# Query stages of a two-layer transformer kernel: order and engine of the weight splits, and loading of the input

## Chip, cores, metric

The kernel runs on one core of one Trainium2 chip. The metric is the device time of one execution in microseconds, the median of several runs.

## The reference

x has 256 tokens (8 sequences of 32) of 512 values. Six blocks are added to it, each on the layer-normalised x. Two of them, the first and the fourth, are cross-attention to a context of 512 positions per sequence, with 32 query heads and 8 key/value heads of 128:

```python
q = (latents @ Wq).reshape(bsz, q_len, HEADS, HEAD_DIM).transpose(0, 2, 1, 3)
k = (kv @ Wk).reshape(bsz, kv_len, KV_HEADS, HEAD_DIM).transpose(0, 2, 1, 3)
v = (kv @ Wv).reshape(bsz, kv_len, KV_HEADS, HEAD_DIM).transpose(0, 2, 1, 3)
q = rms_norm(q, q_norm_w)
k = rms_norm(k, k_norm_w)
...
x = x + _L0_xattn_ref(_layernorm(x, axis=-1), ctx_4096, L0_xattn_Wq, ...)
...
x = x + _L1_xattn_ref(_layernorm(x, axis=-1), ctx_4096, mask_1x1xSxS2_ff0, L1_xattn_Wq, ...)
```

In the first block the latents themselves are keys and values too (`kv` is the context followed by them); the fourth has a mask instead. Everything is float32.

## The kernel before

Each block is a stage, and each stage closes before the next opens. A cross-attention has three: `queries` (tiles named c0q and c1q), `attend` (c0a, c1a) and `project_out`. A float32 product is made of three passes on TensorE (`mm3`, lines 53 to 55), with each operand split in a high part (a copy by ScalarE to fp32r) and a low part (raw minus high, a subtraction). So each weight has to be split before it is used.

`queries` first normalises and transposes x (`LayerNormT`) and splits it (xT). Then Wq goes by in NQ = 8 tiles of 128x2048 (512 output columns, 1 MB) through a two-slot stage (`WeightStream`). For each tile there are TT = 2 projections n (128 tokens each) of 12 matmuls into one of SLOTS = 4 PSUM banks. Each projection n is followed by a chain: ScalarE squares (L490), VectorE sums (L565), GpSimd makes rstd (L406, L409), VectorE normalises into xn (L573), TensorE transposes (L450), ScalarE places the result into qT (L503). LAG = 2 says how many projections later TensorE does the transposes. In c0q four more projections of the latents (keys) with the same chain follow, then four of the latents' values without it, which are stored to DRAM.

Every engine works through its own list in order. In one tile ScalarE's order is: high part of the next wq tile (L194), high part of one key/value weight half (L520), then for each projection square and placing. VectorE's: low part of the next wq tile (L200), then sums and normalise for each projection. GpSimd's: rstd for each projection, then the low part of a key/value half (L413). The key/value weights are four columns of 128x2048 (two for keys, two for values); each is loaded and split in two halves, one per wq tile, so that all four are ready when the stage ends. SyncE's queue: norm weights, then in each tile wq and a key/value half; the context tiles of the first sequence follow the first pair; in c1q the first two wq tiles are already there. The eight tiles are written as a first pair, a loop over two pairs and a last pair (`peeled`). In the last tile both engines split the four context tiles (L273, L278).

`attend` works in 16 units of four context tiles. In a unit without scores yet (the first one) TensorE projects keys (column hf), transposes the normalised keys of the tile before (L831) and projects values (column 2 + hf); the chain of the keys is that of the queries (ScalarE L935, VectorE L1022, GpSimd L753 and L756, VectorE L1038, TensorE L831, ScalarE L906, VectorE L963). With k = 3 its own transposes follow its value projection at once.

`build_program` loads x and the identity in a block of its own, which all engines leave together once both have landed (lines 2213 to 2218), and then opens c0q.

## Time and profile before

| | |
|---|---|
| Runs | 1652.61 us median of 3 (1651.95 to 1656.21) |
| Profiled execution | 1653.78 us, of which span 1651.1 us |
| PE busy | 1524.9 us (92%) |
| DVE busy | 909.1 us (55%) |
| ACT busy | 642.6 us (39%) |
| POOL busy | 374.0 us (23%) |
| Mean granted clock of PE | 0.972 |
| c0q | 5 to 104 us |
| c1q | 816 to 889 us |

PE is TensorE, PEld its weight loads, DVE VectorE, ACT ScalarE, POOL GpSimd, SP SyncE; a q behind the name (PEq, SPq) is the engine's sequencer. A line of a timeline gives the start in us, the length in us, engine, line of the code, operation, output and inputs with their shapes, how many were merged, and in brackets how long the engine was idle before it and what released it. In the busy time by stretch each engine has its busy us and (in brackets) its instructions, then come PE's granted clock (1.00 is 2.4 GHz, 0.50 is 1.2 GHz), the share of time in which the DMA engines were busy, and GB/s. At the very start of c0q the column of the clock reads 1.00 while matmuls take 0.63 us instead of 0.39.

### The profile page before, as it was taken

What the parts mean: (1) busy time and instruction counts of PE and PEld (TensorE: products, weight loads), DVE (VectorE), ACT (ScalarE), POOL (GpSimd) and SP (SyncE); (2) the same over time, 40 slices, a digit from 0 to 9 for tenths busy, and PEclk for the clock granted to TensorE, in tenths of its full rate; (3) what the DMA queues carried; (4) which work ended last, traced back from release to release, by engine and by line L of the source; (5) the groups of instructions that cost most, each with busy time, mean ns of one, the idle gap of its engine ahead of it and who ended that gap; (6) DMA issues with size and microseconds to landing.
All of it is one profiled execution on the core that took longest, in us unless ns stands there. A gap on an engine that the chain in (4) does not pass through costs nothing. (4 is left out here: it accounts for less than half of the span.)

```text
span 1651.1 us, 24177 instructions
## 1 busy us (share of the span) xinstructions
PE 1524.9 (92%) x8362; PEld 1292.3 (78%) x8362; DVE 909.1 (55%) x1707; ACT 642.6 (39%) x1168; POOL 374.0 (23%) x510
## 2 busy tenths in 40 slices
PE   6899999999999998978797999999999999875898
PEld 4678888888888886777576888888888888654787
DVE  5724555555555555575564455555555554547565
ACT  4623343433433434453363333333333333421343
POOL 2622222222122221052355221122222111101000
PEclk9999999999999999989899999999999999988899
DMA  7210000010000111264160000000000001220442
GB/s 251 94 61 20 17 31 17 17 32 14 24 24 11 36 57 52 102 230 154 57 238 7 20 8 25 19 6 25 13 13 25 10 16 74 106 96 1 154 152 90
DMA packets 27371, 99.05 MB, mean 60 GB/s; under 512 B 4977, under 2 KB 5105, under 8 KB 22609
## 3 DMA queue, kind: packets, MB, share of 16 engines
q1 hardware_dynamic: 27312, 98.29, 17.0%
q8 instruction: 34, 0.56, 0.1%
q14 instruction: 25, 0.20, 0.0%
HBM read 95.66 MB, written 2.62 MB: 60 GB/s over the span
## 5 line engine op out<-in xcount | busy, mean ns | idle before, releaser
L53 PE MATMUL c1a_kbanks<-c_wkv_lo_r,c_cT_hi 128*128 128x512 f32 x256 | 106.4, 416 | 3.5 <-PEq L371 3.5
L53 PE MATMUL c0a_kbanks<-c_wkv_lo_r,c_cT_hi 128*128 128x512 f32 x256 | 106.1, 414 | 2.8 <-PEq L371 2.8
L1022 DVE TENSOR_REDUCE c1a_ss<-c1a_sq 128x4 f32<-128x512 f32 x64 | 43.8, 685 | 111.5 <-ACT c1a_sq L935 111.5
L753 POOL TENSOR_TENSOR c1a_ms<-c1a_ss,c1a_const 128x4 f32<-128x4 f32 x64 | 12.7, 199 | 395.2 <-DVE c1a_ss L1022 395.2
L753 POOL TENSOR_TENSOR c0a_ms<-c0a_ss,c0a_const 128x4 f32<-128x4 f32 x64 | 12.7, 199 | 393.4 <-DVE c0a_ss L1022 393.4
L55 PE MATMUL c0a_kbanks<-c_wkv_hi,c_cT_lo_r 128*128 128x512 f32 x256 | 101.2, 395 | 0.0
L55 PE MATMUL c1a_kbanks<-c_wkv_hi,c_cT_lo_r 128*128 128x512 f32 x256 | 100.9, 394 | 0.0
L54 PE MATMUL c0a_kbanks<-c_wkv_hi,c_cT_hi 128*128 128x512 f32 x256 | 100.7, 394 | 0.0
L53 PE MATMUL c0a_vbank<-c_wkv_lo_r,c_cT_hi 128*128 128x512 f32 x256 | 100.6, 393 | 0.0
L54 PE MATMUL c1a_kbanks<-c_wkv_hi,c_cT_hi 128*128 128x512 f32 x256 | 100.5, 392 | 0.0
L54 PE MATMUL c0a_vbank<-c_wkv_hi,c_cT_hi 128*128 128x512 f32 x256 | 100.4, 392 | 0.0
L1022 DVE TENSOR_REDUCE c0a_ss<-c0a_sq 128x4 f32<-128x512 f32 x64 | 43.9, 685 | 102.0 <-ACT c0a_sq L935 93.5
L55 PE MATMUL c1a_vbank<-c_wkv_hi,c_cT_lo_r 128*128 128x512 f32 x256 | 100.0, 391 | 0.0
L53 PE MATMUL c1a_vbank<-c_wkv_lo_r,c_cT_hi 128*128 128x512 f32 x256 | 99.9, 390 | 0.0
L55 PE MATMUL c0a_vbank<-c_wkv_hi,c_cT_lo_r 128*128 128x512 f32 x256 | 99.8, 390 | 0.0
L54 PE MATMUL c1a_vbank<-c_wkv_hi,c_cT_hi 128*128 128x512 f32 x256 | 99.6, 389 | 0.0
L993 DVE COPY c0a_pT<-c0a_ptbank 128x512 f32<-128x512 f32 x62 | 42.9, 692 | 97.8 <-PE c0a_sbank L807 97.8
L917 ACT ACTIVATE c1a_p<-c1a_sm,c1a_nmax 128x512 f32<-128x512 f32 x64 | 46.4, 725 | 128.4 <-DVE c1a_nmax L980 128.4
L917 ACT ACTIVATE c0a_p<-c0a_sbank,c0a_nmax 128x544 f32<-128x544 f32 x62 | 44.4, 716 | 125.8 <-DVE c0a_nmax L973 125.8
L935 ACT ACTIVATE c1a_sq<-c1a_kbanks 128x512 f32<-128x512 f32 x64 | 38.3, 598 | 128.7 <-PE c1a_kbanks L55 128.7
L935 ACT ACTIVATE c0a_sq<-c0a_kbanks 128x512 f32<-128x512 f32 x64 | 38.3, 598 | 119.5 <-PE c0a_kbanks L55 119.5
L993 DVE COPY c1a_pT<-c1a_ptbank 128x512 f32<-128x512 f32 x62 | 42.9, 692 | 75.0 <-PE c1a_ptbank L804 74.8
(469 smaller groups left out, 4417.9 us busy)
## 6 DMA issues: line engine op xcount, KB each, us to landing
g_stage<-in_l_wq SPq DMA_DIRECT2D x16, 1024.0 KB, 4.9
c_cT_lo<-in_ctx SPq DMA_DIRECT2D x64, 256.0 KB, 2.5
c_wkv_lo<-in_l_wo SPq DMA_DIRECT2D x16, 1024.0 KB, 4.9
e_stage<-in_e_w SPq DMA_DIRECT2D x20, 768.0 KB, 4.2
c_wkv_lo<-in_l_wkv SPq DMA_DIRECT2D x16, 512.0 KB, 5.6
m_stage<-in_mix_ffn SPq DMA_DIRECT2D x10, 768.0 KB, 4.5
c_vlat<-vlat_dram SPq DMA_DIRECT2D x32, 64.0 KB, 1.9
m_traw<-in_mix_out SPq DMA_DIRECT2D x1, 1792.0 KB, 12.9
```

The lines of the kernel that those rows point to most:

```text
L53: nc.tensor.matmul(out, a[0], b[1], start=start, stop=False)
L54: nc.tensor.matmul(out, a[0], b[0], start=False, stop=False)
L55: return nc.tensor.matmul(out, a[1], b[0], start=False, stop=stop)
L753: nc.gpsimd.tensor_tensor(ms[:, k % 2, :], ss[:, k % 2, :], const[:, 1, :], ALU.add).then_inc(k_mean, 1)
L917: nc.scalar.activation(dst, src, ACT.Exp, bias=nmax[:, k:k + 1], accum_out=rsum[:, k:k + 1]).then_inc(p_ready, 1)
L935: nc.scalar.activation(sq[:], kbank[k % 2], ACT.Square, scale=HD ** -0.5).then_inc(k_squared, 1)
L993: last = nc.vector.tensor_copy(pT[:, k % 2, :, :], bank[:, :].rearrange("p (t n) -> p t n", t=CT))
L1022: nc.vector.tensor_reduce(ss[:, k % 2, :], sq[:, :].rearrange("p (h d) -> p h d", h=UNIT_H), AX.X, ALU.add).then_inc(k_summed, 1)
```

## The change

- `WeightStream`: each wq tile is split in two halves of 1024 columns, each with its own high part on ScalarE and low part on VectorE. The low part of the first half can start when its high part is done. Both halves still stand ahead of the tile's squares and sums.
- `KeyValueWeights`: the four columns are loaded whole (1 MB each, one semaphore each) beside wq tiles 1 to 4, in the order 0, 1, 2, 3 (c0q) or 0, 2, 1, 3 (c1q). Their halves are split after the second projection of the tiles 3 to 6 (columns one and two of that order). The other two columns follow in c0q beside the four latent projections, in c1a beside the four context tiles of the first unit (`LATE`). The low parts are made by VectorE, no longer by GpSimd; TensorE waits for each column where it first uses it.
- LAG is 3.
- The tiles are written out, without a loop.
- x and ident are loaded at the head of c0q's own queue, with a semaphore each; only VectorE waits for x and only TensorE for ident. The block of its own is gone. The norm weights come behind the first wq tile, the context tiles behind the sixth.
- TensorE's first projections wait for their own half of xT, not for both.
- The split of the context moves: in c0q beside the value projections, in c1q two tiles behind each projection of the last tile.

```diff
...
@@ -171,41 +171,81 @@
 class WeightStream:
...
+    def load(self, sp, src, n):
+
+        need(sp, self.lo_ready, 2 * (n - 1))
+        sp.dma_start(self.stage[:, n % 2, :], src).then_inc(self.loaded[n % 2], 16)
...
+    def make_hi(self, act, n, half, used, per_tile):
+
+        if half == 0:
+            need(act, self.loaded[n % 2], (n // 2 + 1 - self.early) * 16)
+            need(act, used, per_tile * (n - 1))
+        self.nc.scalar.activation(self.part(self.split[0], n, half), self.part(self.stage, n, half),
                                   ACT.Copy).then_inc(self.hi_ready, 1)
...
+    def make_lo(self, dve, n, half):
+        dve.wait_ge(self.hi_ready, 2 * n + half + 1)
+        self.nc.vector.tensor_tensor(self.part(self.split[1], n, half), self.part(self.stage, n, half),
+                                     as_f32(self.part(self.split[0], n, half)),
                                      ALU.subtract).then_inc(self.lo_ready, 1)
...
+    def wait_tile(self, pe, n):
+        pe.wait_ge(self.lo_ready, 2 * n + 2)
...
+    def part(self, ap, n):
...
+    def load(self, sp, i):
+        sp.dma_start(self.raw[:, self.order[i], :], self.src[self.order[i]]).then_inc(self.loaded[i], 16)
+
+    def make_hi(self, act, n):
+        act.wait_ge(self.loaded[n // self.HALVES], 16)
+        self.nc.scalar.activation(self.part(self.split[0], n), self.part(self.raw, n),
+                                  ACT.Copy).then_inc(self.hi_ready, 1)
+
+    def make_lo(self, dve, n):
+        dve.wait_ge(self.hi_ready, n + 1)
+        self.nc.vector.tensor_tensor(self.part(self.split[1], n), self.part(self.raw, n),
+                                     as_f32(self.part(self.split[0], n)), ALU.subtract).then_inc(self.lo_ready, 1)
+
+    def wait_column(self, pe, col):
+        pe.wait_ge(self.lo_ready, self.HALVES * (self.order.index(col) + 1))
+
+    def column(self, col):
+        return tuple(h[:, col, :] for h in self.split)
 
...
-    SLOTS, LAG = 4, 2
+    SLOTS, LAG = 4, 3
+    KV_AT = NQ - 1 - 2 * kvw.HALVES
...
+        def kv_half(n):
+
+            h = n // TT - KV_AT
+            return h if n % TT == 1 and 0 <= h < 2 * kvw.HALVES else None
...
-                sp.dma_start(nk[:, 0:2], w["norm"]).then_inc(small_loaded, 16)
-
-                def step(i):
-                    for slot in range(2):
-                        if not (w["preloaded"] and is_at(i, 0)):
-                            stream.load(sp, w["wq"][bass.ds(2 * i + slot, 1), :, :]
-                                        .rearrange("a p n -> p (a n)"), i, slot)
-
-                        need(sp, wkv_loaded, 16 * (2 * i + slot))
-                        sp.dma_start(wkv_half(2, i, slot).rearrange("p a n -> p (a n)"),
-                                     w["wkv"][bass.ds(i, 1), :, slot * WKH:(slot + 1) * WKH]
-                                     .rearrange("a p n -> p (a n)")).then_inc(wkv_loaded, 16)
-                    if is_at(i, 0):
+                if first:
+                    sp.dma_start(x[:], g["a"]["x"].rearrange("(t p) d -> p t d", p=P)).then_inc(g["x_loaded"], 16)
+                    sp.dma_start(ident[:], g["a"]["ident"]).then_inc(g["ident_loaded"], 16)
+                for n in range(NQ):
+                    if first or n >= 2:
+                        stream.load(sp, w["wq"][n], n)
+                    if n == 0:
+                        sp.dma_start(nk[:, 0:2], w["norm"]).then_inc(small_loaded, 16)
+                    if 1 <= n <= 4:
+                        kvw.load(sp, n - 1)
+                    if n == 5:
                         for k in range(CT):
                             context.load(sp, 0, k)
-                peeled(sp, NQ // 2, step)
...
-                def wkv_lo_of(i, slot):
-                    nc.gpsimd.tensor_tensor(wkv_half(1, i, slot), wkv_half(2, i, slot),
-                                            as_f32(wkv_half(0, i, slot)), ALU.subtract).then_inc(wkv_lo, 1)
...
-                peeled(pool, NQ // 2, step)
-                pool.wait_ge(wkv_hi, NQ)
-                wkv_lo_of(NQ // 2 - 1, 1)
...
             @block.tensor
             def _(pe):
+                if first:
+                    pe.wait_ge(g["ident_loaded"], 16)
                 ln.tensor(pe)
-                ln.wait_ready(pe)
 
...
-                peeled(pe, NQ // 2, step)
+                for n in range(N0):
+                    tile, t = divmod(n, TT)
+                    if tile == 0:
+                        pe.wait_ge(ln.lo_ready, t + 1)
+                    if t == 0:
+                        stream.wait_tile(pe, tile)
+                    need(pe, normed, n - SLOTS + 1)
+                    project(t, stream.tile(tile), pbank[n % SLOTS]).then_inc(projected, 1)
+                    transposes(n - LAG)
...
+                            transposes(NN - LAG + j)
...
-                    transposes(n, n % SLOTS)
+                    transposes(n)
...
-                stream.make_hi(act, 0, 0, projected, TT)
+                for half in range(2):
+                    stream.make_hi(act, 0, half, projected, TT)
                 ln.scalar(act)
...
                 act.wait_ge(norm_ready, 2)
...
+                for n in range(N0):
+                    tile, t = divmod(n, TT)
+                    if t == 0 and tile + 1 < NQ:
+                        for half in range(2):
+                            stream.make_hi(act, tile + 1, half, projected, TT)
+                    square(n)
+                    place(n - LAG)
+                    if kv_half(n) is not None:
+                        kvw.make_hi(act, kv_half(n))
+                    if tile == NQ - 1 and not NL:
+                        for k in (2 * t, 2 * t + 1):
+                            context.make_hi(act, 0, k)
+                for j in range(NL):
+                    square(N0 + j)
+                    place(N0 + j - LAG)
+                    kvw.make_hi(act, 2 * kvw.HALVES + j)
...
+                        context.make_hi(act, 0, j)
                         act.wait_ge(vl_proj, j + 1)
                         if j == 0:
-                            act.wait_ge(stream.lo_ready, NQ)
+                            act.wait_ge(stream.lo_ready, 2 * NQ)
...
-                    stream.make_lo(dve, 0, 0)
+                    for half in range(2):
+                        stream.make_lo(dve, 0, half)
+                if first:
+                    dve.wait_ge(g["x_loaded"], 16)
                 ln.vector(dve, between)
...
+
+                for n in range(N0):
+                    tile, t = divmod(n, TT)
+                    if t == 0 and tile + 1 < NQ:
+                        for half in range(2):
+                            stream.make_lo(dve, tile + 1, half)
+                    sums(n)
+                    normalise(n - 1)
+                    if kv_half(n) is not None:
+                        kvw.make_lo(dve, kv_half(n))
+                    if tile == NQ - 1 and not NL:
+                        for k in (2 * t, 2 * t + 1):
+                            context.make_lo(dve, 0, k)
+                for j in range(NL):
+                    sums(N0 + j)
+                    normalise(N0 + j - 1)
+                    kvw.make_lo(dve, 2 * kvw.HALVES + j)
+                normalise(NN - 1)
+                if NL:
...
+                        context.make_lo(dve, 0, j)
...
+    EARLY = kvw.HALVES * (4 if tail else 2)
+    LATE = kvw.HALVES * 4 - EARLY
...
+                            kvw.wait_column(pe, hf)
                         project(k, hf, kbank[k % 2]).then_inc(k_proj, 1)
                         if lag:
...
+                            kvw.make_hi(act, EARLY + k)
 
                         if hf == 1 and k > 0 and not is_at(b, B - 1):
...
+                            kvw.make_lo(dve, EARLY + k)
                         if lag:
                             ot_place(a - 1, lb, lhf, lk, obank)
...
         stored = s.sem("stored")
         SEMAPHORES.clear()
-        with nc.Block() as block:
-            @block.sync
-            def _(sp):
-                sp.dma_start(x[:], a["x"].rearrange("(t p) d -> p t d", p=P)).then_inc(loaded, 16)
-                sp.dma_start(ident[:], a["ident"]).then_inc(loaded, 16)
-                sp.wait_ge(loaded, 32)
         L0 = {"wkv": a["l0_wkv"], "wq": a["l0_wq"], "wo": a["l0_wo"], "norm": a["l0_norm"], "ctx": a["ctx"], "mask": None,
```

## Rows read from the trace of the kernel before

**Rows 1.** Busy time by stretch (start:end in us, length, engines, clock, DMA).
```profile
46.45:54.19 7.74, 6.95 (x32) 5.25 (x33) 5.60 (x6) 5.10 (x6) 4.76 (x6) 1.00 0.53 197
84.30:87.50 3.20, 3.20 (x18) 2.65 (x17) 1.38 (x2) 1.18 (x2) 2.51 (x5) 1.00 0.02 5
11.00:14.00 3.00, 0.00 (x0) 0.00 (x0) 1.80 (x1) 2.14 (x3) 0.00 (x0) 1.00 0.98 396
824.00:832.00 8.00, 8.00 (x30) 6.38 (x29) 3.20 (x3) 2.36 (x4) 1.21 (x2) 0.81 1.00 376
```

**Rows 2.** Timeline of PE (transposes in c0q) and of ACT (end of c0q).
```profile
46.45 0.66 PE L450 MATMUL c0q_tbank<-g_ident,c0q_xn 128*128 128x128 f32 x4 [1.06 <-DVE c0q_xn L573]
...
100.32 0.60 ACT L543 ACTIVATE g_stage_r<-c0q_pbank 128x512 fp32r<-128x512 f32 x1 [2.10 <-PE c0q_pbank L55]
...
103.04 0.60 ACT L543 ACTIVATE g_stage_r<-c0q_pbank 128x512 fp32r<-128x512 f32 x1 [2.12 <-PE c0q_pbank L55]
```

**Rows 3.** Timeline of DVE: splits of wq tiles in c0q.
```profile
26.64 2.29 DVE L200 TENSOR_TENSOR c0q_w_lo<-g_stage,c0q_w_hi 128x2048 fp32r<-128x2048 f32 x1 [0.52 <-ACT c0q_w_hi L194]
...
33.40 4.07 DVE L200 TENSOR_TENSOR c0q_w_lo<-g_stage,c0q_w_hi 128x2048 fp32r<-128x2048 f32 x1 [1.27 <-ACT c0q_w_hi L194]
...
42.04 3.17 DVE L200 TENSOR_TENSOR c0q_w_lo<-g_stage,c0q_w_hi 128x2048 fp32r<-128x2048 f32 x1 [1.89 <-ACT c0q_w_hi L194]
```

**Rows 4.** Timeline of POOL: one rstd and one key/value subtraction in c0q.
```profile
25.94 1.01 POOL L409 TENSOR_TENSOR c0q_rstd<-c0q_ms,c0q_const 128x4 f32<-128x4 f32 x1
...
32.92 2.40 POOL L413 TENSOR_TENSOR c_wkv_lo_r<-c_wkv_lo,c_wkv_hi 128x1024 fp32r<-128x1024 f32 x1
```

**Rows 5.** Timeline of ACT: high parts of a wq tile and a key/value half.
```profile
47.83 1.91 ACT L194 ACTIVATE c0q_w_hi<-g_stage 128x2048 fp32r<-128x2048 f32 x1
49.63 1.05 ACT L520 ACTIVATE c_wkv_hi<-c_wkv_lo  x1
```

**Rows 6.** Timeline of SPq, ACT, DVE and PE at the start of c0q.
```profile
5.32 0.42 SPq L187 DMA_DIRECT2D g_stage<-in_l_wq  x1
...
10.26 1.91 ACT L194 ACTIVATE c0q_w_hi<-g_stage 128x2048 fp32r<-128x2048 f32 x1 [4.04 <-DMA g_stage<-in_l_wq]
...
12.20 2.29 DVE L200 TENSOR_TENSOR c0q_w_lo<-g_stage,c0q_w_hi 128x2048 fp32r<-128x2048 f32 x1 [3.31 <-ACT c0q_w_hi L194]
...
15.74 0.79 PE L53 MATMUL c0q_pbank<-c0q_w_lo,c0q_xT_hi 128*128 128x512 f32 x1 [5.54 <-DVE c0q_xT_lo L137]
...
21.03 0.59 PE L53 MATMUL c0q_pbank<-c0q_w_lo,c0q_xT_hi 128*128 128x512 f32 x1
```

**Rows 7.** Timeline of PE, ACT and POOL: start and end of c1q.
```profile
823.49 0.80 PE L53 MATMUL c1q_pbank<-c1q_w_lo,c1q_xT_hi 128*128 128x512 f32 x1 [2.14 <-DVE c1q_xT_lo L137]
...
883.16 0.60 ACT L490 ACTIVATE c1q_sq<-c1q_pbank 128x512 f32<-128x512 f32 x1 [1.23 <-PE c1q_pbank L55]
...
887.88 0.69 ACT L503 ACTIVATE c_qT<-c1q_tbank,c1q_norm 128x512 f32<-128x512 f32 x1 [0.57 <-PE c1q_tbank L450]
...
886.38 4.64 POOL L413 TENSOR_TENSOR c_wkv_lo_r<-c_wkv_lo,c_wkv_hi 128x1024 fp32r<-128x1024 f32 x2
...
891.37 0.76 PE L53 MATMUL c1a_kbanks<-c_wkv_lo_r,c_cT_hi 128*128 128x512 f32 x1 [3.52 <-PEq L371]
```

**Rows 8.** DMA issues of 0 to 30 us (KB each, median us to landing).
```profile
g_x<-in_x SPq DMA_DIRECT2D x1, 512.0 KB, 3.6
```

**Rows 9.** Busy time in one microsecond at the start of c1a.
```profile
893.00:894.00 1.00, 1.00 (x3) 0.78 (x3) 0.00 (x0) 0.00 (x0) 0.00 (x0) 0.50 0.43 117
```

**Rows 10.** Timeline of ACT, DVE and PE in the first unit of c1a.
```profile
902.60 0.60 ACT L935 ACTIVATE c1a_sq<-c1a_kbanks 128x512 f32<-128x512 f32 x1
...
905.50 0.69 DVE L1038 TENSOR_TENSOR c1a_kn<-c1a_kbanks,c1a_rstd 128x512 f32<-128x512 f32 x1 [1.47 <-POOL c1a_rstd L756]
...
907.40 0.60 PE L831 MATMUL c1a_ktbank<-g_ident,c1a_kn 128*128 128x128 f32 x4
...
918.08 0.66 PE L831 MATMUL c1a_ktbank<-g_ident,c1a_kn 128*128 128x128 f32 x4 [1.39 <-DVE c1a_kn L1038]
```

More of the change, by code:

```diff
@@ L171, with __init__ @@
 class WeightStream:
-    def __init__(self, nc, s, name, width, stage=None, split=None, preloaded=False):
-        self.nc, self.width, self.ahead = nc, width, int(preloaded)
-        self.stage = stage if stage is not None else s.sb(name + "_stage", [P, 2, width])
-        self.split = split if split is not None else s.pair(name, [P, 2, width])
+    def __init__(self, nc, s, name, width, stage, early):
+        self.nc, self.early, self.half = nc, early, width // 2
+        self.stage = stage
+        self.split = s.pair(name, [P, 2, width])
         self.loaded = [s.sem(f"{name}_loaded{i}") for i in range(2)]
```

203 lines of the change are left out of this document (71 added, 132 removed).

## Prediction

> **What bounds the kernel now.** I read the page first: TensorE is busy 92% of the span and its chain holds the end, so only TensorE's idle time, or its time at the low clock, can be won. The diff touches the two query stages (c0q, 5 to 104 us; c1q, 816 to 889 us), what lies before the first, and the first unit of the attention after each. The busy time by stretches comes next [rows 1]: one weight tile (two projections, two groups of transposes) takes 7.74 us, while the latent part of the same stage does one projection with its transposes in 3.20 us with TensorE busy throughout, so 6.40 us for the same work. The timeline of TensorE says who holds it [rows 2]: once per tile it waits 1.06 us for xn, the normalised queries that VectorE writes. What makes VectorE late stands in its own timeline [rows 3]: the split of the next weight tile takes 2.29 us undisturbed, but 3.17 and 4.07 us where GpSimd subtracts for the key/value weights (2.40 us each [rows 4]). It can start only when ScalarE has written the high part, 1.91 us, behind which ScalarE writes a key/value half for another 1.05 us before it squares [rows 5]. With LAG 2 the transposes come one projection too early for this chain.
>
> **The edits, costed.**
>
> *Tiles of c0q and c1q.* The key/value subtraction leaves GpSimd for VectorE. VectorE's tile was 5.60 us of work; now it is 5.60 - 3.17 + 2.29, and in the tiles 3 to 6 one key/value half more. That half on VectorE is not in the trace; it lies between half of 2.29 us (1.15) and GpSimd's 2.40. The reader and the width are those of the weight split, so I take 1.15: 5.9 us of the 6.40. ScalarE had 5.10 us per tile [rows 1] and keeps it. Cutting 2048 columns into two instructions adds about 0.1 us: 1024 columns take 1.05 us and step by 0.95, 2048 take 1.91 and step by 1.80 [rows 5]. Both have room. The order matters more, so I lay one tile out, with 0 the end of projection 2t-1. ScalarE: square to 0.6, placing to 1.25, key/value half to 2.2, weight halves to 3.15 and 4.1. VectorE: sums to 1.3, normalise to 1.9, key/value half 2.35 to 3.5, weight halves to 4.65 and 5.8. TensorE wants the weights at 6.4 + 0.4 = 6.8, so 1.0 us is left. The transposes now come three projections late: xn(2t-1) is written by 7.1 and asked for at 9.6. What is next late is therefore TensorE itself, at 6.40 us.
> Over c0q: 20 projections with transposes at 3.20, 4 without at 2.72 (the step of the last two [rows 2]), and half of the 5.3 us from 15.74 to 21.03, which run at twice the duration [rows 6]: 64.0 + 10.9 + 2.6 = 77.5 us, against 103.04 - 15.74 = 87.3. I keep 0.3 for pauses: **9.5 us**.
> Over c1q: 12 with and 4 without, 1.8 for the low clock at its start: 51.1 us against 883.16 - 823.49 = 59.7 [rows 7], so 8.6, less 0.3: **8.3 us**.
>
> *Unrolling* the three-body loop costs nothing I can see: no engine idles at a loop edge in these stages. Bound: 0 to 1 us.
>
> *Start of c0q.* The barrier held everything to 4.9 us; the first weight tile was issued at 5.32 and ScalarE could start on it at 10.26 [rows 6]. Now x, ident and the weights follow one another on one queue. x lands 3.6 us after its issue, at about 4.3 [rows 8]; 1 MB behind it at 396 GB/s [rows 1] is 2.6 us more: 7.0 us. Had the two transfers shared the engines evenly it would be 8.5. ScalarE then writes the halves to 8.0 and 8.9; VectorE has finished the LayerNorm by 8.0 (its chain moves only 0.5 us, since it waits for x), subtracts to 9.3 and 10.45, the first xT half to 11.15. TensorE no longer waits for the second xT half. So it starts at 11.2 instead of 15.74 [rows 6]: **4.5 us**, between 3.4 and 5. The norm load now stands behind a weight tile, but is needed at 8.0 and lands at 7. In c1q the tile is preloaded; only the xT half is gained: **0.6 us**.
>
> *Loads.* Each of tiles 2 to 4 now brings 1 MB of wq and 1 MB of key/value weights in 6.4 us, 330 GB/s, against 376 and 396 GB/s reached [rows 1]. A wq tile is issued before the key/value column with it and has more than 7 us until its split. Context loads move behind tile 5; their split moves too, into the last tile (c1q) or beside the value projections (c0q), where both engines are under half busy. Cost 0.
>
> *End of c1q.* GpSimd's last subtractions run from 886.38 for 4.64 us and hold the block open after ScalarE has placed its last queries at 888.57; TensorE begins the attention at 891.37 [rows 7]. That work is gone: 2.4 us. With LAG 3 three groups of transposes are left after the last projection, the last waiting for square, sums, rstd, two context tiles and normalise: last placing 5.25 us after it, against 5.4 now. So 8.3 + 0.6 + 2.4 + 0.2 = **11.5 us** at TensorE's start in c1a. TensorE is nearly idle as long as before this, so I leave its fall to 0.50 of the clock there [rows 9] where it is; if it went, 1.8 us more.
>
> *First unit of c1a.* New: four key/value halves on ScalarE and VectorE, each behind placing and ahead of the next square. The square now starts at 902.60, xn's counterpart kn at 905.50 and ends 906.2; the transposes want it at 907.40 [rows 10]. ScalarE's half pushes the square 0.95, VectorE's half (to 904.8) the sums by 1.5 in all: kn at 907.65, 0.3 late, twice. The fourth transposes follow after one projection only and already wait (918.08, 1.39 us [rows 10]): there 1.5 is paid in full. Queued behind is the score of the next unit. The last column is ready 2.9 us after those transposes and asked for after a 2.7 us projection and a score. **Cost 2.1 us**, between 0.5 and 4.
>
> **Sum** against the profiled execution (1653.78 us, span 1651.1): 9.5 + 4.5 + 11.5 - 2.1 = 23.4, so 1630.4. The median of the runs lies 1.2 below that execution: **1629 us**.
>
> **Where the Trainium skill speaks against it.** VectorE's split at 26.64 takes 2.29 us although GpSimd's rstd (25.94, 1.01 us) is running when it starts [rows 3, 4]: no delay. The skill's "SBUF — State Buffer", section on who interferes with whom, says that a VectorE operation with two SBUF inputs and a GpSimd operation that reads SBUF exclude each other for a whole instruction. By that rule the splits of each key/value tile could lose the 1.0 us of an rstd, and the slack above would be gone; the long pairs (4.07 beside 2.40) agree with it, the short ones do not. By the rule the sum would be that of rival 1, by the row it stays at 1629.
>
> **Rivals.**
> 1. *VectorE becomes the bound in the key/value tiles* (15%). For it: 5.9 of 6.40 us, and a loss of 1.0 us by collision with rstd uses the slack up. Against: the 2.29 us row. Tiles of about 7.2 us, 8 of them: 6.4 us back, 1635.5.
> 2. *The first weight tile lands no sooner than before relative to the barrier* (10%): x, ident and three megabyte loads share the engines. c0q starts at 15, 4 us back: 1633.
> 3. *The weights are not what is late* (the halves stand together ahead of the squares, not between them, and only LAG acts, or only GpSimd's removal, 0.9 us of 1.34 per tile) (5%): 12 tiles by 0.45, 1634.5.
> 4. *Slower: the clock.* (3%) The first projection now starts on less work queued behind it, and c1a starts after thinner transposes. If TensorE stayed at the 0.50 (1.2 GHz) that c1a's start shows [rows 9], each projection would cost 2.7 us more; from 9 projections on the gain is spent, from 11 the kernel is slower by 0.3%, 1658. Against: the waits of 1 to 2 us inside the stages leave the column at 1.00 [rows 1].
>
> **Numbers.** Forecast 67%, from 1624 to 1633 by the bounds of start, first unit and clock. The range 1622 to 1638 takes in the rivals 1 to 3. A measurement of this kernel tells about 0.3% (5 us) from no change: faster 0.94, same 0.03 (rivals 1 and 2 together with a dear first unit), slower 0.03.
>
> **What would show it.** Tiles of 6.4 us and no wait of TensorE for xn in c0q and c1q; VectorE's half splits at 1.15 us; first projection near 11.2; c1a's first projection about 11 us sooner relative to the stage's start; a wait of 2.9 us before the fourth transposes there. Tiles over 7 us, splits over 1.5 us, or waits of TensorE for w_lo would prove it wrong.

## The result, and the profile after

The changed kernel takes 1634.7 us, the median of four executions (1631.66 to 1636.36), beside 1652.28 us for the kernel before on the same chip. The ratio is 0.9888, with an interval of 0.9864 to 0.9912: faster, by 17.6 us (1.1%). The forecast was 1629 us with a range of 1622 to 1638, so the direction and the range held, and the median lies 5.7 us above the forecast.

The profiled execution of after took 1631.66 us, with a span of 1628.8 us and a mean granted clock of 0.971. Against the sum in the forecast (1630.4 us for such an execution) that is 1.3 us off. Two questions follow: does each term of the sum hold, and why does the median lie higher than the profiled execution, when it lay 1.2 us below it for the kernel before?

The busy time of each engine, from the page of after:

```profile
PE 1521.6 (93%) x8362; PEld 1293.1 (79%) x8362; DVE 913.2 (56%) x1739; ACT 642.7 (39%) x1184; POOL 335.4 (21%) x494
```

GpSimd gave up 38.6 us, and VectorE took only 4.1 us more: 16 key/value halves of 1.23 us came to it (19.7 us), while its own splits are no longer stretched. TensorE has the same number of matmuls (8362).

One tile of c0q with a key/value half, as busy time by stretch (start:end, length, PE, PEld, DVE, ACT, POOL, clock, DMA share, GB/s). It answers to the 7.74 us of [rows 1]:

```profile
39.97:46.44 6.47, 6.47 (x34) 5.32 (x33) 6.00 (x8) 5.08 (x8) 2.41 (x5) 1.00 0.29 95
```

TensorE is busy for all 6.47 us, VectorE for 6.00 and ScalarE for 5.08. The same tile in the timelines of VectorE and GpSimd (for [rows 3] and [rows 4]):

```profile
39.97 1.23 DVE L241 TENSOR_TENSOR c_wkv_lo_r<-c_wkv_lo,c_wkv_hi 128x1024 fp32r<-128x1024 f32 x1 [0.24 <-ACT c_wkv_hi L236]
41.11 2.36 DVE L202 TENSOR_TENSOR c0q_w_lo<-g_stage,c0q_w_hi 128x1024 fp32r<-128x1024 f32 x2
...
39.55 1.01 POOL L442 TENSOR_TENSOR c0q_rstd<-c0q_ms,c0q_const 128x4 f32<-128x4 f32 x1
```

A tile's low part now takes 2.36 us in place of 3.17 and 4.07, and the key/value half 1.23. The rstd that runs when the half begins does not stretch it.

The start of c0q, timeline of VectorE, ScalarE and TensorE (for [rows 6]):

```profile
4.57 1.29 DVE L125 BATCH_NORM_STATS2 c0q_ln_stats<-g_x 128x6 f32<-128x512 f32 x2 [4.57 <-DMA g_x<-in_x]
...
7.26 2.01 ACT L197 ACTIVATE c0q_w_hi<-g_stage 128x1024 fp32r<-128x1024 f32 x2 [5.24 <-DMA g_stage<-in_l_wq]
...
11.41 0.79 PE L53 MATMUL c0q_pbank<-c0q_w_lo,c0q_xT_hi 128*128 128x512 f32 x1 [1.55 <-DVE c0q_xT_lo L137]
```

The end of c1q, timeline of ScalarE and TensorE (for [rows 7]): the square of the last projection, the last placing, the first projection of the attention.

```profile
859.05 0.60 ACT L506 ACTIVATE c1q_sq<-c1q_pbank 128x512 f32<-128x512 f32 x1 [1.02 <-PE c1q_pbank L55]
...
863.97 0.69 ACT L516 ACTIVATE c_qT<-c1q_tbank,c1q_norm 128x512 f32<-128x512 f32 x1 [1.56 <-PE c1q_tbank L465]
...
865.12 0.77 PE L53 MATMUL c1a_kbanks<-c_wkv_lo_r,c_cT_hi 128*128 128x512 f32 x1 [1.19 <-PEq L408]
```

The first unit of c1a, timeline of ScalarE, VectorE and TensorE (for [rows 10]):

```profile
882.22 0.60 ACT L927 ACTIVATE c1a_kT_hi<-c1a_ktbank 128x512 fp32r<-128x512 f32 x1 [2.94 <-PE c1a_ktbank L848]
882.71 1.05 ACT L236 ACTIVATE c_wkv_hi<-c_wkv_lo 128x1024 fp32r<-128x1024 f32 x1
883.66 0.59 ACT L956 ACTIVATE c1a_sq<-c1a_kbanks 128x512 f32<-128x512 f32 x1
...
883.79 1.23 DVE L241 TENSOR_TENSOR c_wkv_lo_r<-c_wkv_lo,c_wkv_hi 128x1024 fp32r<-128x1024 f32 x1 [0.26 <-ACT c_wkv_hi L236]
884.93 0.68 DVE L1045 TENSOR_REDUCE c1a_ss<-c1a_sq 128x4 f32<-128x512 f32 x1
887.08 0.69 DVE L1061 TENSOR_TENSOR c1a_kn<-c1a_kbanks,c1a_rstd 128x512 f32<-128x512 f32 x1 [1.47 <-POOL c1a_rstd L773]
...
887.83 0.66 PE L848 MATMUL c1a_ktbank<-g_ident,c1a_kn 128*128 128x128 f32 x4 [0.17 <-DVE c1a_kn L1061]
894.12 0.66 PE L848 MATMUL c1a_ktbank<-g_ident,c1a_kn 128*128 128x128 f32 x4 [2.90 <-DVE c1a_kn L1061]
```

Each half stands ahead of the square on ScalarE and ahead of the sums on VectorE. TensorE waits 0.16 to 0.17 us for kn twice, and 2.90 us before the fourth transposes.

What the clock did at the two stage borders and after them, as busy time by stretch of after:

```profile
88.00:97.00 9.00, 6.05 (x27) 4.71 (x26) 1.12 (x2) 1.20 (x2) 0.14 (x2) 1.00 0.59 233
...
859.00:867.00 8.00, 4.54 (x22) 3.30 (x20) 3.08 (x5) 4.05 (x7) 1.89 (x5) 0.71 0.11 24
...
894.00:899.00 5.00, 4.88 (x24) 4.11 (x25) 2.78 (x5) 2.95 (x4) 0.00 (x0) 1.00 0.02 3
```

The clock stays at 2.4 GHz into c0a, where the kernel before fell:

```profile
107.00:111.00 4.00, 4.00 (x12) 3.13 (x12) 0.00 (x0) 0.60 (x1) 0.00 (x0) 0.60 0.91 358
```

That row is of the kernel before, at the start of its c0a (first projection at 105.80).

**Where the 22.3 us between the spans (1651.1 and 1628.8) come from.** The same event was read in both traces and the two starts subtracted:

| event | before | after | gained so far |
|---|---|---|---|
| first projection of c0q | 15.74 | 11.41 | 4.3 |
| ScalarE's last copy of c0q (latents' values) | 103.04 | 89.31 | 13.7 |
| last write into c0a's key banks (transposes in its last unit) | 647.0 | 631.7 | 15.3 |
| c1q begins (its LayerNorm's transposes) | 819.4 | 803.3 | 16.1 |
| first projection of c1a | 891.37 | 865.12 | 26.3 |
| first output product of c1a | 928.4 | 904.4 | 24.0 |
| last output product of c1o | 1465.5 | 1442.6 | 22.9 |

### The profile page after: what moved, and what is told of

The parts are those of the page before. It is cut to its first block and busy times, and to the rows that moved or that the text cites. A ratio compares the mean times of both kernels' runs of the same rounds, so it can differ in the third digit from the quotient of the medians.

```text
span 1628.8 us, 23964 instructions
## 1 busy us (share of the span) xinstructions
PE 1521.6 (93%) x8362; PEld 1293.1 (79%) x8362; DVE 913.2 (56%) x1739; ACT 642.7 (39%) x1184; POOL 335.4 (21%) x494
```

## The experiments

**The theory.** In the query stages TensorE waited for xn. The shorter VectorE chain and the later transposes (LAG 3) together put the tile at TensorE's own 6.4 us. The start, the tail of c1q and the dearer first unit of c1a make up the rest. **The rivals** that were still alive: only LAG or only GpSimd's removal acts; halves against whole tiles matters; the start is hidden anyway. After the result one more: the granted clock at the borders decides the last few microseconds. Times are medians of four to six executions; every ratio is to the kernel before on the same chip, with its interval.

| run | us | ratio |
|---|---|---|
| e1, after again | 1634.22 | 0.9891 [0.9876, 0.9907] |
| e2, LAG 2 in after | 1638.24 | 0.9910 [0.9895, 0.9925] |
| e3, key/value halves back on GpSimd | 1639.67 | 0.9927 [0.9913, 0.9940] |
| e4, both | 1649.3 | 0.9973 [0.9961, 0.9986] |
| e5, only LAG 3 in before | 1640.71 | 0.9931 [0.9917, 0.9944] |
| e6, square and sums before the half | 1634.91 | 0.9891 [0.9876, 0.9907] |
| e7, whole tiles | 1633.53 | 0.9882 [0.9867, 0.9898] |
| e8, barrier back | 1635.8 | 0.9903 [0.9888, 0.9919] |
| e9, after again, beside e10 to e12 | 1634.28 | 0.9880 [0.9863, 0.9896] |
| e10, half behind kn | 1631.74 | 0.9867 [0.9852, 0.9882] |
| e11, TensorE kept busy at the borders | 1630.55 | 0.9864 [0.9849, 0.9879] |
| e12, e10 and e11 | 1627.6 | 0.9849 [0.9836, 0.9863] |

### Which part carries the tiles: e1 to e5

e1 is the changed kernel unchanged but for a blank line, to have it beside the others.

> The changed kernel once more, unaltered, to see what differs between two executions of it. Its runs so far went from 1631.7 to 1636.4 us, wider than those before the change. Theory A (the clock): the granted clock falls to 0.50 or not at the change from c0q to c0a (in the first profiled execution it did not: column 1.00 from 88 to 97 us, while before the change it stood at 0.50 from 107 to 110), and the span follows by about 1.7 us for each such stretch gained or lost. Then stage lengths in this trace equal those of the first except where the clock differs. Theory B: something else (the landing of the stored latent values, 8 us) varies; then the first unit of c0a moves with the clock at 1.00 all the same.

It gave 1634.22 us (1630.88 to 1636.18), and its stages start within 1 us of those of after throughout. The trace of after can be reproduced, but it isn't typical: both traces are the fastest of their four executions. The clock stayed up at the start of c0a in both, so the two don't decide between the theories; e9 below bears theory A out, with a fall there that cost 1.3 us.

e2 takes back LAG alone:

```diff
-    SLOTS, LAG = 4, 3
+    SLOTS, LAG = 4, 2
```

> The changed kernel with LAG 2 in place of 3, nothing else. Theory A (mine: both parts act): with the key/value half on VectorE xn(2t-1) is ready 0.65 us after TensorE wants to transpose it, so the eight key/value tiles go from 6.47 to 7.2 to 7.4 us and the others stay at 6.5: 6 to 8 us slower than the changed kernel, and waits for xn appear in tiles 3 to 6 only. Theory B (the work taken from GpSimd is what counted, LAG is idle): within 1 us. Theory C (LAG is all): every tile goes back to 7.7, 17 us slower.

e3 keeps LAG 3 and gives the key/value low parts back to GpSimd, each after a normalisation's rstd:

```diff
-    def make_lo(self, dve, n):
-        dve.wait_ge(self.hi_ready, n + 1)
-        self.nc.vector.tensor_tensor(
+    def make_lo(self, pool, n):
+        pool.wait_ge(self.hi_ready, n + 1)
+        self.nc.gpsimd.tensor_tensor(
...
+                    if n < N0 and kv_half(n) is not None:
+                        kvw.make_lo(pool, kv_half(n))
```

> The changed kernel with the low parts of the key/value halves back on GpSimd, behind the rstd of the same projection, LAG 3 kept. Theory A: VectorE's split beside GpSimd's 2.40 us is stretched from 1.15 to 2.3 us and more per half, weights come 0 to 1 us later than TensorE asks for them: 0 to 8 us slower. In c1a the 1.15 us on VectorE ahead of the sums falls away, 1 us faster there. Theory B (GpSimd's removal is all of the gain): tiles of 7.7, 17 us slower. Theory C (LAG is all): within 1 us.

e4 makes both edits.

> Both undone: key/value low parts on GpSimd and LAG 2. If the two parts are what made the tiles short, the key/value tiles are back at 7.5 to 7.8 us, the tiles without key/value work at 6.5 to 6.8 (before the change every tile had a half): 10 to 13 us slower than the changed kernel. If the order of the halves or the unrolling did it, the tiles stay under 6.8 and it is less than 4 us slower.

e5 goes the other way: the kernel before, with its loop, its barrier and its GpSimd work, and only LAG changed.

```diff
-    SLOTS, LAG = 4, 2
+    SLOTS, LAG = 4, 3
```

> The kernel before the change with LAG 3 in place of 2, nothing else. Theory A (both parts act): TensorE no longer waits for xn, but GpSimd's 2.40 us still stretch VectorE's split, so now TensorE waits for w_lo, as in e3, whose key/value tiles took 7.23 us. Here every tile has a half: tiles of 7.2 instead of 7.74 us, 7 us faster than before over 14 tiles, waits for w_lo instead of xn. Theory C (LAG is all): tiles of 6.5, 17 us faster. Theory B (only GpSimd's removal helps): within 1 us of before.

Measured: e2 costs 4.0 us (6 to 8 expected), e3 5.5 us (0 to 8) and e4 15.1 us (10 to 13) against e1 in the same series: together 5.6 us more than the two alone. Read from e4, the work taken from GpSimd gives 11.1 us with LAG 2 (e2) and LAG 3 gives 9.6 us with GpSimd's work kept (e3): either one alone brings about two thirds of the 15.1 us, and the other then adds only 4.0 to 5.5. e5 alone gains 11.7 us (7 expected), where e1 gains 18.6. The stages themselves, from the traces: in c0q from the first projection to the start of the last matmul, in c1q from its first projection to the first of c1a, and the first unit of c1a up to its first output product.

| us | before | e5 | e4 | e3 | e2 | after |
|---|---|---|---|---|---|---|
| c0q | 86.9 | 77.8 | 84.1 | 79.3 | 80.0 | 77.5 |
| c1q and its tail | 67.9 | 62.5 | 64.7 | 60.4 | 60.2 | 58.3 |
| first unit of c1a | 37.0 | 36.7 | 42.3 | 42.0 | 41.2 | 39.3 |

What TensorE waits for, in timelines of TensorE: first e4 (LAG 2, GpSimd), then e2 (LAG 2, VectorE), then e3 (LAG 3, GpSimd).

```profile
47.04 1.11 PE L469 MATMUL c0q_tbank<-g_ident,c0q_xn 128*128 128x128 f32 x4 [2.17 <-DVE c0q_xn L592]
```

```profile
45.66 0.65 PE L465 MATMUL c0q_tbank<-g_ident,c0q_xn 128*128 128x128 f32 x4 [0.48 <-DVE c0q_xn L588]
```

```profile
44.46 0.50 PE L53 MATMUL c0q_pbank<-c0q_w_lo,c0q_xT_hi 128*128 128x512 f32 x1 [0.55 <-DVE c0q_w_lo L202]
```

With LAG 2 the wait is for xn; the lighter VectorE shortens it from as much as 2.17 to 0.48 us but does not end it. With LAG 3 the wait for xn is gone in c0q in all of them; behind the last projection of c1q it stays (2.2 to 2.4 us in after, e3 and e5). What is next late then depends on VectorE: in e3 it is the low part, 0.5 us per tile. The reason stands in VectorE's and GpSimd's timelines of e3:

```profile
40.16 4.25 DVE L202 TENSOR_TENSOR c0q_w_lo<-g_stage,c0q_w_hi 128x1024 fp32r<-128x1024 f32 x2 [1.18 <-ACT c0q_w_hi L197]
...
39.78 2.41 POOL L241 TENSOR_TENSOR c_wkv_lo_r<-c_wkv_lo,c_wkv_hi 128x1024 fp32r<-128x1024 f32 x1
```

The same two subtractions take 2.36 us in after. The 1.89 us more are most of GpSimd's 2.41: the two engines took turns, as in [rows 3, 4], and VectorE waited, since GpSimd had begun first. In the next tile of e3 VectorE begins first, but GpSimd's half comes in between VectorE's two (timeline of VectorE, then GpSimd, of e3):

```profile
47.07 4.56 DVE L202 TENSOR_TENSOR c0q_w_lo<-g_stage,c0q_w_hi 128x1024 fp32r<-128x1024 f32 x2
...
47.66 2.89 POOL L241 TENSOR_TENSOR c_wkv_lo_r<-c_wkv_lo,c_wkv_hi 128x1024 fp32r<-128x1024 f32 x1
```

In e5 VectorE also begins first, with the whole tile in one instruction, and now GpSimd pays (timeline of VectorE, then GpSimd, of e5):

```profile
38.89 2.28 DVE L200 TENSOR_TENSOR c0q_w_lo<-g_stage,c0q_w_hi 128x2048 fp32r<-128x2048 f32 x1
45.73 2.29 DVE L200 TENSOR_TENSOR c0q_w_lo<-g_stage,c0q_w_hi 128x2048 fp32r<-128x2048 f32 x1 [0.34 <-ACT c0q_w_hi L194]
...
39.47 3.95 POOL L413 TENSOR_TENSOR c_wkv_lo_r<-c_wkv_lo,c_wkv_hi  x1
45.89 4.39 POOL L413 TENSOR_TENSOR c_wkv_lo_r<-c_wkv_lo,c_wkv_hi  x1
```

So LAG 3 did more in e5 than ask later: from 38.89 on VectorE's splits are back at 2.28 and 2.29 us (3.17 and 4.07 in [rows 3]), and the delay fell on GpSimd (3.95 and 4.39 us for 2.40), which has room inside c0q. That is how e5 comes within 0.3 us of after there and e3 does not; TensorE waits only once in e5 between 30 and 80 us, for 0.46 us. That the cut into halves is what lets GpSimd in between is read from these rows and was not tried by itself: no run has whole tiles with LAG 3 and the other edits of the change, but GpSimd's subtractions kept.

Where e3 loses its time: 1.8 us in c0q, 2.1 in c1q and 2.7 in the first unit of c1a. In that unit 1 us less was expected; instead each rstd queues behind a half of 2.40 us on GpSimd, and TensorE waits 0.6 us for kn twice and then 3.30 us. e5, apart from its later start, loses most at the end of c1q (3.6 us), where it still has its last subtractions open, and after doesn't (timeline of GpSimd, then TensorE, of e5):

```profile
871.46 4.65 POOL L413 TENSOR_TENSOR c_wkv_lo_r<-c_wkv_lo,c_wkv_hi 128x1024 fp32r<-128x1024 f32 x2
...
876.45 0.76 PE L53 MATMUL c1a_kbanks<-c_wkv_lo_r,c_cT_hi 128*128 128x512 f32 x1 [3.07 <-PEq L371]
```

The subtractions end at 876.11 and c1a's first projection follows at 876.45.

### Halves or whole tiles, and the barrier: e7, e8

e7 splits each wq tile in one instruction again, in the places of after:

```diff
-                        for half in range(2):
-                            stream.make_hi(act, tile + 1, half, projected, TT)
+                        stream.make_hi(act, tile + 1, 0, projected, TT)
...
-                        for half in range(2):
-                            stream.make_lo(dve, tile + 1, half)
+                        stream.make_lo(dve, tile + 1, 0)
```

> The changed kernel with each wq tile split by one instruction of 2048 columns on each engine again, in the same place. Theory A (order and load of the engines matter, the halves hardly do): VectorE starts 0.95 us later on each tile, within the 1.0 us to spare, so tiles stay at 6.5 us; only the start of c0q is 0.8 us later. 0.5 to 1.5 us slower. Theory D (the halves are what lets the weights be in time): waits for w_lo in each key/value tile, 5 us slower or more.

It took 1633.53 us (0.5 to 1.5 us slower expected), no different from e6 (1634.91) and e1. Its first projection is 0.8 us later (12.2), for ScalarE and VectorE no longer overlap on the first tile, yet the last matmul of c0q starts at 89.0, as after's does at 88.9. Cutting the wq tiles is worth nothing that these runs can show.

e8 loads x and the identity behind a barrier again:

```diff
+        with nc.Block() as block:
+            @block.sync
+            def _(sp):
+                sp.dma_start(x[:], a["x"].rearrange("(t p) d -> p t d", p=P)).then_inc(g["x_loaded"], 16)
+                sp.dma_start(ident[:], a["ident"]).then_inc(g["ident_loaded"], 16)
+                sp.wait_ge(g["x_loaded"], 16)
+                sp.wait_ge(g["ident_loaded"], 16)
```

> The changed kernel with x and ident loaded again in a block of their own, that all engines leave together. By my sum the first projection goes from 11.4 to 15.2 us: 3.5 to 4.3 us slower, the rest unchanged. If the loads of 1 MB key/value columns are what limits the first tiles, the difference is smaller than the shift of the first projection.

Timeline of ScalarE and TensorE of e8:

```profile
10.06 2.00 ACT L197 ACTIVATE c0q_w_hi<-g_stage 128x1024 fp32r<-128x1024 f32 x2 [3.60 <-DMA g_stage<-in_l_wq]
...
14.17 0.80 PE L53 MATMUL c0q_pbank<-c0q_w_lo,c0q_xT_hi 128*128 128x512 f32 x1 [3.71 <-DVE c0q_xT_lo L137]
```

The first weights arrive 2.8 us later than in after, and so does the first projection. The stage ends 2.1 us later (91.0 against 88.9). The median is 1.1 to 1.6 us above those of after, e1 and e9, less than the trace says, less than the 3.5 to 4.3 that were expected, and too small to tell from none in these runs. The other 1.6 us of the 4.3 at the start (15.74 - 14.17) come without the barrier's removal: 0.8 are the halves (e7), and the rest is put down to TensorE no longer waiting for the second half of xT, which no run takes back alone.

### The first unit of c1a: e6, e10

e6 puts the square before ScalarE's key/value half and the sums before VectorE's:

```diff
                         nc.scalar.activation(sq[:], kbank[k % 2], ACT.Square, scale=HD ** -0.5).then_inc(k_squared, 1)
+                        if is_at(b, 0) and hf == 0 and k < LATE:
+                            kvw.make_hi(act, EARLY + k)
...
                                                 AX.X, ALU.add).then_inc(k_summed, 1)
+                        if is_at(b, 0) and hf == 0 and k < LATE:
+                            kvw.make_lo(dve, EARLY + k)
```

> The changed kernel; in the first unit of c1a ScalarE's key/value half stands behind the square of its context tile (where ScalarE waits 1.7 us for the value projection anyway) instead of ahead of the next one, and VectorE's half between the sums and the normalising (where VectorE waits 1.47 us for rstd). If the order costs the 6.30 us steps of that unit (5.92 before) and the 2.9 us wait before its fourth transposes, the steps are back at 5.9, that wait at 1.4, and the kernel is 2.0 to 2.3 us faster than the changed one. If it is the amount of work or the loads of those columns, nothing changes.

The keys' transposes step by 5.93 us again (878.96, 884.89, 890.82), where after had 6.31. But the median did not move: 1634.91 us. In e6 the half now runs between sums and rstd, and GpSimd's tiny addition pays (timeline of GpSimd and VectorE of e6):

```profile
881.66 1.29 POOL L770 TENSOR_TENSOR c1a_ms<-c1a_ss,c1a_const 128x4 f32<-128x4 f32 x1 [3.02 <-DVE c1a_ss L1045]
...
881.66 1.22 DVE L241 TENSOR_TENSOR c_wkv_lo_r<-c_wkv_lo,c_wkv_hi 128x1024 fp32r<-128x1024 f32 x1 [0.15 <-ACT c_wkv_hi L236]
```

Alone that addition takes 0.20 us. Beside the half it takes 1.29, so kn is late by as much, and the fourth transposes wait 2.5 us instead of the 1.4 that the edit was to bring. That is 1.1 of the expected 2.2 us. The other part is the clock. In e6's trace it falls behind that wait, as busy time by stretch:

```profile
896.00:901.00 5.00, 4.33 (x14) 3.60 (x15) 1.31 (x2) 0.60 (x1) 0.46 (x1) 0.66 0.01 3
```

From the fourth to the fifth transposes e6 needs 8.69 us (896.67 to 905.36), after 7.10. So its first unit takes 39.8 us in the trace, where after takes 39.3.

e10 therefore puts VectorE's half behind kn, ScalarE's as in e6:

```diff
                             ALU.mult).then_inc(k_normed, 1)
+                        if is_at(b, 0) and hf == 0 and k < LATE:
+                            kvw.make_lo(dve, EARLY + k)
                         if attends:
                             pt_copy(a, k, ptbank, sbank)
```

Its control is e9, the changed kernel once more in the same series:

> The changed kernel unaltered, as the control for the three beside it on the same chip: 1634 to 1635 us median, runs from 1631 to 1636. The mean clock and the span of the runs go together, about 0.004 of clock for 5 us, if the number of falls of the clock is what spreads them.

> Like e6, but VectorE's key/value half in the first unit of c1a stands behind the normalising instead of ahead of it. In e6 GpSimd's addition for rstd took 1.29 us beside that half, 0.20 without, so the normalising came late by another engine's wait. Theory A (that collision is what kept e6 from its gain): GpSimd's addition is back at 0.20, steps of 5.9 us, wait before the fourth transposes 1.4 us, 2.2 us less than the changed kernel between the start of c1a and its second unit where the clock is alike. Theory B (the collision is harmless): as e6.

e10 took 1631.74 us against 1634.28 for e9, 2.5 us less; the intervals of the two ratios overlap, so the medians alone would not show it. Timeline of GpSimd and VectorE of e10:

```profile
882.51 0.20 POOL L770 TENSOR_TENSOR c1a_ms<-c1a_ss,c1a_const 128x4 f32<-128x4 f32 x1 [3.89 <-DVE c1a_ss L1045]
...
883.83 0.69 DVE L1061 TENSOR_TENSOR c1a_kn<-c1a_kbanks,c1a_rstd 128x512 f32<-128x512 f32 x1 [1.47 <-POOL c1a_rstd L773]
884.43 1.22 DVE L241 TENSOR_TENSOR c_wkv_lo_r<-c_wkv_lo,c_wkv_hi 128x1024 fp32r<-128x1024 f32 x1
```

The addition is back to 0.20 us, VectorE's half stands where VectorE has nothing else to do, and the wait before the fourth transposes is 1.4 us. That is the cost of the first unit (2.3 us in after) taken back: in the e10 trace 37.0 us lie between the first projection of c1a (869.7) and its first output product (906.7), as in the kernel before (891.4 to 928.4), against 39.3 in after.

The shorter wait has a second effect. Here are the fourteen traces by the wait before the fourth transposes, and whether the granted clock fell behind it:

| wait, us | traces | clock fell in |
|---|---|---|
| 1.39 to 1.41 | before, e5, e10, e12 | none |
| 2.50 to 3.30 | after, e1, e2, e3, e4, e6, e7, e8, e9, e11 | e2, e4, e6, e8, e9, e11 |

So e10's order also takes away the wait behind which the clock falls in six traces of ten.

### The clock at the borders: e11, e12

e11 lets TensorE multiply into a free bank, with results that nobody reads, while it waits at the end of c0q and between the last transposes of c1q:

```diff
+                def idle_work(count):
+                    a = tuple(h[:, 0, 0:P] for h in xT)
+                    wt = stream.tile(NQ - 1)
+                    for _ in range(count):
+                        nc.tensor.matmul(pbank[0][:], a[0], wt[0][:, 0:UW], start=True, stop=True)
...
+                    pe.wait_ge(vl_rest, 1)
+                    idle_work(5)
                     return
+                idle_work(3)
                 for n in range(NN - LAG, NN):
                     transposes(n)
+                    idle_work(4)
```

> The changed kernel with matmuls whose results nobody reads, where TensorE idles at the end of the query stages: 5 behind the last projection of c0q, and 3, 4, 4 and 4 around the last three groups of transposes of c1q. They lie beside the last work of ScalarE and VectorE, so the stages end when they did, or up to 0.5 us later. Theory A (the idle time at the ends of the stages is what lets the clock fall, and the falls spread the runs): the column stays at 1.00 where c1a begins (0.50 from 863 to 869 us in the first trace of the changed kernel), 1.5 to 2.2 us less there, in every run; falls at the start of c0a become rarer; median 1630 to 1633. Theory B (the falls have another cause, or cost nothing): the median stays at that of the control or 0.5 us above it.

e12 is e10 and e11 together:

> Both of e10 and e11: if each holds, 2.2 and 1.5 to 4 us, 1628 to 1630 us, the fastest so far. If a fall of the clock is only moved to the next idle stretch, no better than e10.

e11 took 1630.55 us, 3.7 below e9. e12 took 1627.6 (1626.32 to 1628.3), 6.7 below e9: the fastest of all, 1.5% below the kernel before. The two gains (2.5 and 3.7) add up to 6.2. Of the three only e12 stands, just, clear of e9 (0.9836 to 0.9863 beside 0.9863 to 0.9896); the interval of e11 overlaps with it. The clock in c1a, as busy time by stretch, first e11 at the start and behind the fourth transposes, then e12 at the start and at the end of the first unit:

```profile
862.00:870.00 8.00, 7.54 (x37) 5.78 (x36) 2.25 (x5) 3.08 (x6) 1.70 (x4) 1.00 0.14 35
...
894.00:899.00 5.00, 5.00 (x17) 3.98 (x16) 2.01 (x3) 2.19 (x4) 0.00 (x0) 0.66 0.00 0
```

```profile
859.00:867.00 8.00, 7.55 (x39) 5.76 (x38) 3.03 (x5) 3.48 (x6) 1.90 (x5) 1.00 0.13 35
...
894.00:899.00 5.00, 5.00 (x28) 4.20 (x27) 2.63 (x6) 2.38 (x5) 2.42 (x3) 1.00 0.15 52
```

At the start the column reads 1.00 where after reads 0.71. From there to the fourth transposes e11 needs 27.1 us, after 29.0: 1.9 us gained. But behind its wait of 2.88 us e11's clock fell, and 1.6 us were lost again (8.67 us to the fifth transposes, 7.10 in after). e12, which has neither the low clock at the start nor the long wait, needs 35.2 us for the first unit, 1.8 less than e10. So 1.8 to 1.9 us of e11's 3.7 are seen at this place in traces. At c0a's start the matmuls prove nothing: the clock stays up there in e11 and e12, but also in after, e1, e3 and e8 without them.

What the clock costs when it falls shows in e9, which is the same program as after, on the same stretch:

```profile
894.00:899.00 5.00, 3.83 (x11) 3.23 (x12) 2.49 (x3) 1.55 (x2) 0.95 (x2) 0.54 0.00 0
```

After had 1.00 here. In between lie the 2.90 us of waiting at the fourth transposes: in after the clock stayed up behind them, in e9 it fell. e9 begins its fourth transposes 1.05 us behind after (895.17, 894.12) and its fifth 3.89 us behind (905.11, 901.22), so this fall cost 2.8 us. Another one, at the start of c0a, cost e9 1.3 us (it is 0.6 behind at the first key projection and 2.0 behind at the last). The wait before it was 2.95 us in e9 and 2.94 in after. These two are the largest losses but not the whole account of the 4.7 us between the spans (1633.5 and 1628.8): e9 makes up 0.9 us between the first projections of c1q and c1a and 1.2 us in c1o, and loses 1.9 us more behind c1o.

## Why the prediction was right, and where it was off

**What bounds.** Right. The wait for xn is gone in c0q, the tile takes 6.47 us where 6.40 was forecast, and TensorE is busy throughout. VectorE has 6.00 us of work in the tile (5.9 forecast). In c1q two waits for xn are left (2.3 us together), both behind the last projection.

**Tiles of c0q: 9.5 us.** Measured 13.7 - 4.3 = 9.4. The size was right; that both edits were needed for it was not, in this stage: e5 has 9.1 of it from LAG alone. The forecast read the gap of 1.34 us per tile as a VectorE that is too busy. It was one of order in two ways: TensorE asked for the transposes one projection too early, and GpSimd began its subtraction before VectorE's. With LAG 3 alone the second turned round as well, and VectorE's splits were no longer stretched (2.29 us in e5). Rival 3 (only LAG acts) was nearer to this stage than its 5% said, but its time (1634.5, with 12 tiles losing 0.45 us) was worked out from a loss that e5 does not show in c0q. It falls for the whole kernel, since e5 gains 6.9 us less than e1. In its traces those are the start (4.5), the tail of c1q (3.6) and the tiles of c1q and c0q (0.9), less the 2.6 us by which e5's first unit of c1a is shorter.

**Halves between normalisations.** The forecast gave the cutting itself a cost of 0.1 us, and e7 shows a worth of about nothing beyond the first tile.

**Start: 4.5 us.** Measured 4.3: x at 4.57 (4.3 forecast), weights at 7.26 (7.0), first projection at 11.41 (11.2). e8 gives 2.8 of them to the barrier, and in the median little of that can be seen.

**c1q: 11.5 us.** Measured 26.3 - 16.1 = 10.2. Of this 0.6 is the start, as forecast. From the first projection to the last square it is 7.5 instead of 8.3 (59.67 to 52.21 us): six tiles with 6.47 for 6.40 are 0.4 of the 0.8. The other 0.4 is the low clock at the stage's start, which the forecast put at 1.8 us and which lasted longer: the mean granted clock of the first 5 us is 0.57 in after and 0.65 before. From the last square to c1a it is 2.1 instead of 2.6 (8.21 to 6.07): the last placing ends 5.61 us after the last square begins, where the forecast had 5.25 and the kernel before 5.41, so the 0.2 us that LAG 3 was to give there were lost instead. This is the largest miss of the sum, and it is one of size.

**First unit of c1a: 2.1 us lost.** Measured 2.3 (26.3 - 24.0), by the mechanism that was named: steps of 6.31 instead of 5.92 us, then 2.90 us of waiting where 2.9 was forecast. e10 takes it away by order alone. What the forecast did not see is that the unit had room for the halves all along, behind kn. Nor did it price its own 2.9 us of waiting for the clock: the rows it leant on have waits of 1 to 2 us with the column at 1.00, and behind this longer one the clock fell in six traces of ten.

**What was left out of the sum.** The clock at the start of c0a, 0.60 before and 1.00 in after, gave 1.6 us (13.7 to 15.3); that it stayed up is chance too, since it falls there in e6, e7, e9 and e10. What lies between c0a and c1q gave 0.8 (to 16.1), and c1o took 1.1 back, by the clock at its start (0.50 and 0.79 over 1396 to 1400 and 1400 to 1404 us in after, 0.61 and 0.96 over 1420 to 1424 and 1424 to 1428 us before). Together they are +1.3, which makes good the misses above: 23.4 - 0.1 - 0.2 - 1.3 - 0.2 + 1.3 = 22.9, against 22.9 at the end of c1o and 22.3 at the end of the span. Part of the good agreement of the sum with the profiled execution is therefore luck.

**Why the median lies 5.7 us above.** 1.3 of them are the sum's miss and 0.2 rounding; 4.2 are a step that the forecast took without an argument: the median was put 1.2 us below the profiled execution because the kernel before had it so, and it lies 3.0 above. Executions of the changed kernel differ in how often the clock falls behind a wait. In after, e1 and e9 together, the two with a mean clock of 0.972 or more took 1629.86 and 1630.88 us, and the three with 0.968 took 1635.84 to 1636.36; the seven between lie anywhere from 1631.66 to 1636.21, for a fall costs time only where TensorE has work, and the mean doesn't see where it lands (0.971 for both profiled executions, of after and of e9). The profiled execution of after was the best of its four, and that it was the one with the trace is luck. e9's falls, priced above, are most of the difference to it; e12, whose clock holds at both ends of c1a's first unit, has its five executions within 2.0 us, while after, e1 and e9 spread over 4.7 to 6.4. That falls of the clock spread the executions is shown for the two with a trace (after and e9). For the others it is argued from the mean clock, and e12 changes TensorE's idle time along with the clock.

**Rival 4 (the clock)** came true in kind and not in size: the first unit of c1a lost 2.8 us to it in e9, about what one projection loses at 1.2 GHz, where nine would have been needed to spend the gain. The clock came back to 2.4 GHz each time.

**Rival 1 and the Trainium skill.** By the Trainium skill's page "SBUF — State Buffer", section on who interferes with whom, the VectorE halves could lose to each rstd. The row at 39.97 shows 1.23 us beside a running rstd, as e10's 1.22 alone: VectorE did not lose here, so the rule's sum did not come. e6 shows the rule from the other side: GpSimd's 128x4 addition took 1.29 us, the length of the VectorE half beside it, in place of 0.20. Long pairs exclude each other in either direction: VectorE 4.25 us beside a 2.41 us subtraction that began first (e3), GpSimd 3.95 and 4.39 us beside a 2.29 us one that began first (e5). For e6 against e10 the rule accounts for 1.1 us of the 2.8 between their first units (39.8 and 37.0); 1.6 are the clock.

## What to carry to other kernels

When an engine waits for a chain, there are two ways out, and they can stand in for each other: ask one step later, or take work off the chain. One more step of lag gave 11.7 of 18.6 us here with no work moved (e5), and moving the work gave 11.1 us with the old lag (e2 against e4). The lag is the smaller edit where the buffers allow it, so try it first, and don't add up the two. When two engines exclude each other, look at which begins first and where the other can come in between: e3 loses 0.5 us per tile because one subtraction holds up the other, and e5, where they meet in another order, loses nothing. When work is moved onto a chain, put it behind the chain's last product, not merely "after the square": of two tries in the same unit, one brought nothing and the other 2.5 us in the median. And a sum that fits one profiled execution to a microsecond says little about the median of a kernel whose waits stand where the clock may fall; shorten those waits, keep the engine fed there (1.8 to 1.9 us at c1a's start), or widen the range.

## What the hardware showed that was not expected

- A GpSimd addition of 128x4 elements takes 0.20 us alone and 1.29 us when a VectorE subtraction of 128x1024 elements from two SBUF inputs (1.22 us) starts with it, while the same kind of subtraction starting beside a running rstd of 128x4 elements takes 1.23 us and is not stretched.
- Of two VectorE and GpSimd subtractions with SBUF inputs the one that begins second waits for the first: VectorE takes 4.25 us for 2.36 when GpSimd began 0.4 us earlier (e3), GpSimd 3.95 us for 2.40 when VectorE began 0.6 us earlier (e5).
- Of two executions of one program, one kept TensorE at 2.4 GHz behind a wait of 2.9 us and one fell to a granted clock of 0.54 over the next five microseconds, at 2.8 us. Over all traces the clock fell behind this wait in six of ten where it was 2.50 to 3.30 us, and in none of four where it was 1.4 us. Such a wait is thus no fixed cost but a chance of one.
- Matmuls whose results nobody reads kept the clock up: in e11 and e12 the column reads 1.00 over c1a's start, where every trace without them has a stretch at 0.50, and the stage gains 1.8 to 1.9 us there.
